# A load on a busy DMA queue, moved: the parts of the weights go behind the denominators and the residual's row instead of ahead of them

## What is computed

```
qk  = einsum('bhdq,bhdl->bhql', qh, kh) * scale
sm  = softmax(qk, axis=-1)
ret = einsum('bhql,bhdl->bhdq', sm, vh)
out = gamma * ret          # times tanh(gate), added to x
```

## Time and profile before

| what | us |
|---|---|
| median of 3 runs | 728.2 |
| profiled execution, its own time | 727.5 |
| its span | 725.4 |
| PE busy | 685.0 (94%) |
| DVE busy | 524.1 (72%) |
| ACT busy | 540.3 (74%) |
| POOL busy | 481.2 (66%) |
| `mx`, 256 maxima on DVE | 296.4 |
| exponentials, 512 on ACT | 279.3 |

### The profile page before, as it was taken

How to read it: one execution, slowest core, us unless ns; L and a number is a source line. 1 busy time by engine, 2 the same in 40 slices (tenths; PEclk the granted TensorE clock), 3 DMA queues, 4 the chain that set the end, 5 groups by cost and what they waited for, 6 DMA issues and landing times.

```text
span 725.4 us, 20869 instructions
## 1 busy us (share of the span) xinstructions
PE 685.0 (94%) x6101; PEld 372.5 (51%) x6101; DVE 524.1 (72%) x853; ACT 540.3 (74%) x1129; POOL 481.2 (66%) x474
## 2 busy tenths in 40 slices
PE   1799999999999999999999999999999999999998
PEld 0122223223333333222355555688888888888744
DVE  3989999999999999999779667544444444444456
ACT  2399999899999999999885866677667676767411
POOL 3557689888888888895668443156566666666622
PEclk9999999999999999999999999999999999999999
DMA  6655576566556665564155745789888888877487
GB/s 203 203 158 179 182 236 204 170 219 207 190 194 206 218 206 173 198 200 151 54 158 175 271 162 176 218 137 180 118 121 116 129 125 108 106 101 97 53 265 272
DMA packets 136865, 123.98 MB, mean 171 GB/s; under 512 B 70612, under 2 KB 106196, under 8 KB 136792
## 3 DMA queue, kind: packets, MB, share of 16 engines
q1 hardware_dynamic: 121928, 106.58, 51.1%
q0 software_dynamic: 13632, 15.47, 15.2%
q10 hardware_dynamic: 1232, 0.98, 0.4%
HBM read 60.33 MB, written 51.53 MB: 154 GB/s over the span
## 4 chain that ended last, share of the span: by engine, by line
PE 77%; DVE 9%; issue 4%; DMA 3%; ACT 3%; SPq 2%; ACTq 0%; DVEq 0%; POOL 0%
PE EH L1296 27%; PE Y L1296 17%; PE pv L561 14%; PE ring L548 9%; DVE mx L707 6%; PE nat L536 5%; ACT P L632 2%; DVE statx L688 1%; PE ring L580 1%; PE ring L571 1%; SPq L396 1%; DMA k_scratch<-khl 1%; DMA q_scratch<-qhl 1%; DMA dc<-den_scratch 1%; PE Y L1509 0%
## 5 line engine op out<-in xcount | busy, mean ns | idle before, releaser
L707 DVE TENSOR_REDUCE mx<-nat 128x2 f32<-128x1024 f32 x256 | 296.4, 1212 | 22.9 <-PE nat L536 21.9
L632 ACT ACTIVATE P<-ring 128x512 f32<-128x512 f32 x512 | 279.3, 603 | 20.3 <-PE ring L548 10.3
L2092 POOL DMA_INDIRECT y_sums<-ysb,to x84 | 138.4, 1647 | 95.9 <-DVE ysb L2029 82.8
L561 PE MATMUL pv<-P,VT 128*32 128x256 f32 x2048 | 158.7, 394 | 0.4
L536 PE MATMUL nat<-KS,QS 48*128 48x512 f16 x512 | 112.2, 398 | 23.2 <-DMA QS<-q_scratch 13.8
L548 PE MATMUL ring<-QS,KS 49*128 49x512 f16 x512 | 124.5, 393 | 8.7 <-ACT P L632 8.7
L1642 ACT ACTIVATE X<-EH,bcur 128x256 f32<-128x256 f32 x168 | 85.6, 559 | 50.9 <-DVE u L1993 50.5
L1296 PE MATMUL Y<-whi,u 128*128 x672 | 117.1, 273 | 0.5 <-DVE u L1993 0.5
L1296 PE MATMUL EH<-XA,whi 128*128 128x256 f16 x672 | 116.9, 273 | 0.3 <-DMA XA<-g_rows 0.3
L1993 DVE TENSOR_TENSOR u<-X,u 128x512 f16<-128x512 f32 x84 | 57.7, 686 | 78.5 <-ACT u L1648 76.7
L1296 PE MATMUL EH<-XA,wlo 128*128 128x256 f16 x336 | 91.6, 273 | 0.0
(11 more groups left out here) (266 smaller groups left out, 993.1 us busy)
## 6 DMA issues: line engine op xcount, KB each, us to landing
XA<-in_wall SPq DMA_DIRECT2D x8, 800.0 KB, 4.4
u<-in_wall SPq DMA_DIRECT2D x8, 800.0 KB, 4.4
QS<-q_scratch SPq DMA_DIRECT2D x64, 96.0 KB, 2.5
KS<-k_scratch SPq DMA_DIRECT2D x62, 96.0 KB, 2.2
X<-in_x SPq DMA_DIRECT2D x16, 256.0 KB, 2.9
q_scratch<-qhl SPq DMA_DIRECT2D x16, 256.0 KB, 2.1
xr<-in_x SPq DMA_DIRECT2D x16, 256.0 KB, 3.6
rd<-den_scratch SPq DMA_DIRECT2D x16, 256.0 KB
```

Of the source, the lines that this page charges most:

```text
L561: m = pe.matmul(pv[32 * j:32 * j + 32, q], VT[i][:, lb, g, j, :], Pb[4 * (s % 2) + j][:, q], start=(lb == 0 and half == 0), stop=(lb == 3) ...
L632: act.activation(Pb[4 * (s % 2) + j][:, :], bank[:, :], ACT.Exp).then_inc(t_use.sem, 1)
L707: dve.tensor_reduce(mx[:, k // 8, :, k % 8], nat[k % 2][:, :, :], AX.X, ALU.max).then_inc(t_max.sem, 1)
L2092: pool.indirect_dma_start(out=ysum[:, :], out_offset=bass.IndirectOffsetOnAxis(ap=to[:, j % 2, a:a + 1], axis=0), in_=ysb[j % 2][:, a, :], ...
```

## The change

Step 3 of the list moves behind step 5. Nothing else changes: the same instructions, the same waits, the same bytes.

```diff
                     sp.dma_start(sd[ck.index(t), 0]...[g], U[g][r:P:32, :]).then_inc(t_ds.sem, 16)
-            if 2 <= w < B - 1:
-                load_weights(ck, w + 1)
             if t >= 0:
                 ck.wait(t_ds, t)
                 ck.wait(t_dve, t - 1, "recip")
...
             if t >= 0:
                 ck.wait(t_pool, t - 1, "x1")
                 sp.dma_start(xr[:, :], x[ck.index(t)]).then_inc(t_xr.sem, 16)
+            if 2 <= w < B - 1:
+                load_weights(ck, w + 1)
             if 0 <= w < B - 2:
                 load_ctx(ck, w + 2)
```

## The result

The changed kernel takes **742.6 us**, the median of five runs (737.21 to 744.59), against 728.2 us before. The ratio is 1.0181, with a 95% interval from 1.0154 to 1.0208: slower by 1.8%. The profiled execution is the lowest of the five, 737.21 us with a span of 735.1 us. It is compared with the profile of before first (9.7 us between the two); what the other runs add to it comes with the experiments. In experiments 5 and 7 one execution each, of 1631 and 3573 us, lies far off all the others and is left out of the times given.

The account below looks back on a forecast made before the run. SP's round of transfers was to become the bound in place of DVE's and PE's work: 2.9 + 6.6 - 1.3 = 8.2 us slower, 735.7 from the profiled 727.5, forecast 736 for the median. Range 727 to 744.

Parts of the forecast that it names:

- The bound: In the attention loop, SP's round exceeds DVE's 20.71 us window once the lead passes about 10.0 us.
- lead: SP's longest link, from the store of the denominators to the first load of KS: 9.97 us in window 6, 8.91 in window 8.
- the slack: SP's waits in window 8 for `qhl` (0.8 us) and U (0.3 us), about 1.1 us a window that a longer lead can use up.
- The new lead: Denominators' store to KS after the change: `xr` landed at 6.0 us, weights 8.8, context and `khl` 10.7, KS at 10.95.
- The sum: Loss over the loop: 2.9 us in windows 4 to 6, 6.6 in windows 7 to 13, less 1.3: 8.2 us slower.
- PE's reserve: At PE's start on the new stacks, QS may come 1.28 us later once before PE stands; takes 1.3 us off.
- second part of the lead: The weights behind `xr`: 4.4 us alone less 1.6 us that even `dc` needs, so 2.8 us of transfer, landing at 8.8.
- bound of 11.75 us: Highest lead, with a train as slow as window 6's 8.3 us from weights to KS: 16 us slower, 744.
- the prediction's own prices: Loss counted as lead above 9.97 us in three windows and above 8.91 plus 1.1 us in seven, less 1.3 us.
- What was worth nothing: DVE's 1.1 us wait for `dc` in windows 4 and 5 vanishes inside the new wait and gives nothing.
- The train did not keep up: Rival: SP's transfers near the best rate, lead under 10.0 us, not slower, 728.2 down to 725.8; chance 0.25.
- the other rival: PE's clock falls to 1.2 GHz in each window, 0.35 us more for about ten windows, 740; chance 0.15.

Follow-up runs that it names:

- experiment 5: Against the changed kernel, each weights part in two 400 KB halves, one ahead of the wait for the denominators' store, one behind `xr`: 729.8 us, ratio 1.0024.
- experiment 7: Against the changed kernel, the weights go further back, behind the two stores of the keys and ahead of the issue of KS: 728.2 us, ratio 1.0010.
- experiment 1: Against the changed kernel, the weights are issued at the end of each window, behind the last KS and QS stacks: 731.1 us, ratio 1.0054.
- experiment 8: Against the changed kernel, weights directly behind `dc` and the residual's row behind the store of the keys (windows 2 to 13): 730.6 us, ratio 1.0043.
- experiment 2: Against the changed kernel, the weights stand behind `dc` and ahead of `xr`: 736.8 us, ratio 1.0135.
- experiment 6: The changed kernel again, unedited, with a profile of a slower execution of 747.79 us: 743.7 us, ratio 1.0206.
- Experiment 4: The changed kernel plus five small matmuls with unused output on PE ahead of its wait for the stacks, windows 4 to 14: 741.4 us, ratio 1.0175.

## Why the prediction was right

*The bound.* "The lead may grow from 8.9 to about 10.0 us before SP's round is longer than DVE's window": the table has the mean lead of windows 7 to 13, and the time from the first maximum of window 7 to that of window 15, eight windows.

| kernel | mean lead, us | eight windows, us |
|---|---|---|
| experiment 7 | 8.82 | 165.0 |
| before | 9.01 | 165.6 |
| experiment 1 | 9.56 | 168.0 |
| experiment 8 | 9.61 | 165.6 |
| experiment 5 | 10.15 | 165.7 |
| experiment 2 | 10.88 | 170.5 |
| changed | 11.07 | 172.2 |

Experiment 1 alone is out of order, for the reason given there. The engine waits in the earlier trace rows were the slack and vanished as forecast.

*The new lead.* It was added up as 10.95 us; the ten windows of the profiled run have 10.94 to 11.36 us, mean 11.08. The parts hold as well: in window 6 `xr` had landed 6.2 us after the store (6.0 forecast), the weights at 9.2 (8.8), the keys at 10.8 (10.7). One reason given for it was not right: the part of the weights does not move while SP waits for the store to land. In the kernel before it begins to move when that wait is over, and what the change adds is a later start of the train (in window 6 4.5 us after the store and not 2.9), less what the train is shorter (6.4 us from its start to the landing of the keys and not 6.8).

The Trainium skill's rule in "DMA: Bandwidth & Descriptors" (Anatomy of one DMA), 2.0 us plus the bytes at 436 GB/s, gave an estimated lead of 9.7 us and no loss, and 11.08 us were measured. That section gives the rule for one DMA issued by GpSimd, and these are five issued by SyncE; the measurement shows that it does not carry over to this train.

*The sum.* It was 2.9 us up to window 6, 6.6 us for the next seven, and -1.3 for PE's reserve. X of window 7 was late by 3.4 us, of which 1.0 arose ahead of the loop, where I had counted nothing, and 2.4 in windows 4 to 6. From there to X of window 13 six windows lost 7.3 us, 1.2 each and not 0.94: their rounds take 21.8 us in the mean where 21.65 was forecast, 0.12 of it by the longer lead, and before they had taken 20.63 us from X to X, a little under the 20.71 of DVE. By the store of the denominators of window 14 the loss was 10.4 us; at the first maximum of window 15 9.3, so PE's reserve was 1.1. The sum of 8.2 us became 9.7 in this execution. That 736 lies so near to its 737.2 us is in part luck, since the terms were off in both directions.

*The step that was too small* is the second part of the lead. The weights' "alone they land 4.4 us after issue" was taken from a place where X, the last bulk load ahead of them, goes out 2.4 us earlier and has nearly landed (in window 6 at 143.41 us, with the weights issued at 142.94). By the sum they would land 4.7 us after their issue; directly behind `xr` they need 5.0 us in the median, and up to 6.6 in the slower run. There the mean lead is 11.5 us, near the bound of 11.75 us, "a train that is as slow as that of window 6", which gave 744. By the prediction's own prices 11.5 us make 13.8 us of loss, 742. That execution lost 20.3, and the rest lies where the sum has no term: the store of the queries in window 4, and the windows with the clock at 0.50 at the end of the attention and behind it (experiment 6). The median, 742.6, is nearer to the upper end of the range than to the forecast of 736, and no trace is of an execution near it: how its 14.4 us divide between late transfers and the clock stays open.

*What was worth nothing.* `dc` landed 2 us earlier, its wait was gone, and the new wait at the start of the window swallowed it, as said.

*The rivals.* The train did not keep up (lead 11.1 and not under 10.0 us). The clock fell three times in the attention of the profiled run, as the other rival wanted, if not in each window. Here is one of the falls in the view by stretches, as in the earlier trace rows:

```profile
207.90:211.20 3.30, 3.30 (x23) 0.55 (x17) 3.22 (x5) 1.76 (x4) 3.05 (x4) 0.50 0.57 156
```

This rival's time, 740, lies nearer to the median than the forecast does, so the time does not tell the two apart. Experiment 4 does: with the falls nearly gone, 13 of the 14 us stay. In windows where SP's round is longer than DVE's the falls of the first trace add nothing that can be seen; in window 14 of the slower execution one added 2.4 us.

## What to carry to other kernels

An engine that issues transfers in strict order forms a loop of its own; compare the round of that loop, with its waits for landings, with the window of the busiest engine, and know the slack before a bulk load is moved. In this kernel the issue of a bulk load ahead of a wait for a small transfer's landing was free, since the time to its first bytes ran in that wait. The same 800 KB cost nothing there or behind the store of the keys (experiment 7), and 14 us between the two. When a load can only stand in the train, count it at the time that it takes directly behind another load, not at the time that it takes alone.

## What was unexpected

A part of 800 KB that follows another bulk transfer without a gap often has some of the 16 DMA engines 1 to 3 us behind the first one to finish. Of the 13 parts that the body issues in windows 2 to 14, the landing took 4.4 us in the median and 4.9 at the most before, 4.5 and 4.9 behind `dc` (experiment 2), 5.0 and 5.6 to 6.6 behind `xr`, 5.1 and 7.4 behind the keys. Why that is, and why it falls on some windows of an execution and not on others, stays open. Giving the stacks a shorter way by fewer bytes, which would show whether the 11.1 us could be had in all runs, was not tried.
